# A graph layer in three blocks: message and node stages joined, and four operations moved

## Chip, cores and metric
The kernel runs on one core of a Trainium2 chip. The metric is the device time of one execution in microseconds, the median of several runs. Trainium2's engines work in parallel and meet at semaphores: PE (TensorE, matmuls and transposes), DVE (VectorE), ACT (ScalarE), POOL (GpSimd) and SP (SyncE, which here only starts DMAs). Each runs its own instructions strictly in the order written.

## What is computed
```python
h = maximum(layernorm(x), 0)                      # x: 50000 x 256
Q, K, V = h @ Wq, h @ Wk, h @ Wv                  # 8 heads of 32
scores = einsum('ehd,ehd->eh', Q[dst], K[src]) * SCALE    # 12500 edges, sorted by dst
w = exp(scores - max over the edges of a dst);  w = w / (sum over them + 1e-8)
out[dst] += V[src] * w
out = layernorm(h + out @ Wo_w + Wo_b, g1, b1)
ffn = gelu(out @ ffn_w1 + ffn_b1) @ ffn_w2 + ffn_b2       # 256 -> 512 -> 256
return x + layernorm(out + ffn, g2, b2)
```

## The kernel before
All numbers are float32. For accuracy a matmul of float32 data is done as three of fp32r data: each operand is split into a high part (a rounded copy, mostly made on ACT) and a low part (the difference, made on DVE), and hi*hi, hi*lo and lo*hi are summed in PSUM.

**Score stage** (`score_stage`). 25 groups of 512 edges. POOL gathers the rows of x for the dst side ("d") and src side ("s") by indirect DMA; DVE takes statistics (`statistics`, `inverse_root`), ACT normalises, PE transposes into the PSUM tile a_T, ACT and DVE split (`high_part`, `low_part`), PE forms Q, K and V. `products` and `head_sums` on DVE make the scores. V stays in SBUF as `vt`. a_T serves both sides in turn, so PE's transposes of side 1 wait for `low_part` of side 0. SP also fills agg_scratch in HBM with the bias of Wo.

**Softmax stage** (`softmax_stage`): scans over the sorted edges, untouched by the change.

**Message stage** (`message_stage`). 25 groups of 512 edges. SP loads alpha (the weights, 16 rows) and cont (does this edge continue its dst?); ACT casts alpha (L652); PE spreads it over the head dimensions into c_A (L587); DVE multiplies by vt (L632) and sums within a dst by a scan (L639); PE multiplies the totals by Wo (L599); ACT copies to c_rows (L657), four buffers; POOL scatters the rows to agg_scratch, four indirect DMAs a group (L682). The block ends when every scatter has landed.

**Node stage** (`node_stage`), a block of its own. First weights and vectors are loaded (L764 to L767), the weights are scaled and split on DVE (L845 to L852). Then 98 groups of 512 nodes; step s of the loop works on several groups at once:
- POOL adds agg_scratch to z of group s+3 by an accumulating DMA (L806), and b2 to x (L807); it makes u = zn*g1 + b1 + fb2 for group s+1 (L813, L815) and the reciprocal roots (L802, L828).
- ACT normalises z of group s+1 to zn (L943) and x of group s+4 with ReLU (L954); for group s it applies gelu in PSUM to the four chunks c of 128 hidden features (L963), makes act_hi (L968), seeds Y with u (L985); for group s+1 it makes zt_hi, the high part of the transposed zn, in two halves (L973).
- PE: for group s four chunks of six d_F matmuls (L1031), then the transposes of group s+1, half 0 (L1018), the d_Y matmuls of chunks 0 and 1 (L1042), the transposes of half 1, the d_Y matmuls of chunks 2 and 3. d_F has three banks, so chunk 3 takes the bank of chunk 0 and waits for act_lo 0; T is one bank, so half 1 waits for zt_lo 0.
- DVE: statistics (L887, L890), centring (L894) and output (L879) of group s-1; act_lo of group s (L857), zt_lo of group s+1 (L863); statistics of z for s+2 (L900, L909) and x for s+5 (L904, L913, L918).

The order of all of this is written out by hand in the loops over s.

Of the kernel before, what the change touches and what calls it, by code (L numbers as in the profile page):

```python
# [18 lines left out]
P = 128  # L19
# [70 lines left out]
def score_stage(nc, x, ends_cols, wq, wk, wv, wo_b, vt, score_dram, agg_dram):  # L90
    with ExitStack() as ctx:
# [56 lines left out]
        with nc.Block() as block:  # L148
# [38 lines left out]
            def _(dve):  # L187
# [68 lines left out]
                for s in range(FIRST, EG):  # L256
# [7 lines left out]
                    else:  # L264
                        statistics(s + 2)
                        products(s)
                        head_sums(s)
                        low_part(s + 1, 0)
# [251 lines left out]
def message_stage(nc, dst_cols, next_cols, wo, wo_b, vt, alpha_dram, cont_dram, agg_dram):  # L520
    with ExitStack() as ctx:
# [10 lines left out]
        w = sb("c_wo", [P, KD, D])  # L532
# [7 lines left out]
        msg = [sb(f"c_msg{r}", [P, KD, GR]) for r in range(2)]  # L540
        total = [sb(f"c_total{r}", [P, KD, GR]) for r in range(2)]
        rows = [sb(f"c_rows{r}", [P, GT, D]) for r in range(4)]
        A = [ctx.enter_context(nc.psum_tensor(f"c_A{r}", [P, KD, GR], f32)) for r in range(2)]
        Y = [ctx.enter_context(nc.psum_tensor(f"c_Y{r}", [P, GT, D], f32)) for r in range(2)]
# [7 lines left out]
        FIRST = -3  # L552
        with nc.Block() as block:
            @block.sync
            def _(sp):
                sp.dma_start(dst[:], dst_cols).then_inc(loaded, 16)
                sp.dma_start(nxt[:], next_cols).then_inc(loaded, 16)
                sp.dma_start(w[:], wo.rearrange("(k p) n -> p k n", p=P)).then_inc(loaded, 16)
# [11 lines left out]
                for c in range(FIRST, EG):  # L570
                    step(Step(c))

            @block.tensor
            def _(pe):
# [4 lines left out]
                def step(s):  # L579
# [9 lines left out]
                    if s.exists(EG):  # L589
# [7 lines left out]
                        for j in range(GT):  # L597
                            for k in range(KD):
                                ins = nc.tensor.matmul(Y[r][:, j, :], total[r][:, k, j * P:(j + 1) * P], w[:, k, :],  # L599
                                                       start=False, stop=(k == KD - 1), skip_group_check=True)  # L600
                        ins.then_inc(y_done, 1)
                for c in range(FIRST, EG):
                    step(Step(c))

            @block.vector
            def _(dve):

                dve.wait_ge(loaded, 64)
                nc.vector.tensor_tensor(same[:], dst[:], nxt[:], ALU.is_equal).then_inc(same_done, 1)
                dve.wait_ge(same_done, 1)  # L610
                nc.vector.scalar_tensor_tensor(row_of[:], same[:], float(SKIP), dst[:], ALU.mult, ALU.add)\
                    .then_inc(index_done, 1)
                dve.wait_ge(consts, 9)
                nc.vector.tensor_tensor(spread[:], spread_part[0][:], spread_part[1][:], ALU.add).then_inc(prep, 1)
                nc.vector.tensor_copy(ones[:], ones_raw[:]).then_inc(prep, 1)
                nc.vector.tensor_copy(bias_hi[:], bias_raw[:]).then_inc(prep, 1)
                dve.wait_ge(prep, 3)
                nc.vector.tensor_tensor(bias_raw[:], bias_raw[:], bias_hi[:].bitcast(f32), ALU.subtract).then_inc(prep, 1)
                nc.vector.tensor_scalar(bias_part[:], bias_hi[:].bitcast(f32), pick[:, 0:1], None, ALU.mult).then_inc(prep, 1)
                dve.wait_ge(prep, 5)  # L620
                nc.vector.scalar_tensor_tensor(bias[:], bias_raw[:], pick[:, 1:2], bias_part[:], ALU.mult, ALU.add)\
                    .then_inc(prep, 1)

                def step(s):
                    if s.exists(EG):
                        r = s.c % 2
                        dve.wait_ge(group_in[s.c % 4], s.use(4, 32))
                        if s.after(2):
                            dve.wait_ge(y_done, s.times(1, -1))
                        for c in range(KD):  # L630
# [10 lines left out]
                for c in range(0, EG):  # L641
                    step(Step(c))
# [466 lines left out]
```

## Time and profile before
| | us |
|---|---|
| median of 3 runs | 1828.78 (1828.08 to 1831.19) |
| the profiled execution | 1828.51 |
| its span, first to last instruction | 1826.8 |
| PE busy in it | 1650.9 (90%) |
| DVE | 1515.3 (83%) |
| POOL | 1295.5 (71%) |
| ACT | 1280.9 (70%) |

The score stage takes the first 310 us or so, the softmax until 362, the messages until 534, the nodes the rest. Busy shares are averages over these stages. Matmuls are pipelined and overlap in the records: PE counts as busy from one to the next if the gap is short, so the start-to-start spacing says more than the share.

### The profile page before, as it was taken

What the parts mean: (1) busy time and instruction counts of PE and PEld (TensorE: products, weight loads), DVE (VectorE), ACT (ScalarE), POOL (GpSimd) and SP (SyncE); (2) the same over time, 40 slices, a digit from 0 to 9 for tenths busy, and PEclk for the clock granted to TensorE, in tenths of its full rate; (3) what the DMA queues carried; (4) which work ended last, traced back from release to release, by engine and by line L of the source; (5) the groups of instructions that cost most, each with busy time, mean ns of one, the idle gap of its engine ahead of it and who ended that gap; (6) DMA issues with size and microseconds to landing.
All of it is one profiled execution on the core that took longest, in us unless ns stands there. A gap on an engine that the chain in (4) does not pass through costs nothing.

```text
span 1826.8 us, 31063 instructions
## 1 busy us (share of the span) xinstructions
PE 1650.9 (90%) x10411; PEld 1441.2 (79%) x10411; DVE 1515.3 (83%) x4604; ACT 1280.9 (70%) x2366; POOL 1295.5 (71%) x1313
## 2 busy tenths in 40 slices
PE   4899997299803999999999999999999999999997
PEld 4888887167702888888888888888888888888886
DVE  3888885677503899999999999999999999999986
ACT  3777775022203888888888888888888888888884
POOL 7777640057734777878878778778778778788783
PEclk8999999589955999999999999999999999999999
DMA  5899895034326677767777777777777677677761
GB/s 161 263 299 303 292 267 196 26 101 135 113 86 167 135 165 171 170 167 166 173 168 162 176 171 162 171 174 164 167 171 170 165 169 170 167 165 173 169 129 57
DMA packets 133619, 309.48 MB, mean 169 GB/s; under 512 B 14622, under 2 KB 69614, under 8 KB 133460
## 3 DMA queue, kind: packets, MB, share of 16 engines
q0 software_dynamic: 42624, 139.33, 37.8%
q1 hardware_dynamic: 90836, 168.17, 27.6%
q8 instruction: 83, 1.36, 0.3%
q14 instruction: 76, 0.62, 0.1%
HBM read 140.66 MB, written 118.20 MB: 142 GB/s over the span
## 4 chain that ended last, share of the span: by engine, by line
PE 67%; DMA 1%; DVE 1%; POOL 1%; ACT 0%; SPq 0%; issue 0%; DVEq 0%; POOLq 0%; ACTq 0%
PE d_F L1031 31%; PE d_Y L1042 31%; PE d_T L1018 6%; DMA d_fb_row<-in_fb 1%; PE d_Y L1008 0%; DMA d_z<-agg_scratch 0%; ACT d_zn L943 0%; PE d_F L1001 0%; SPq L767 0%; POOL d_zx_rstd L828 0%; POOL d_u L815 0%; POOL d_u L813 0%; ACT d_z L954 0%; DVE d_y_stats L887 0%; DVE d_zx_stats L900 0%
## 5 line engine op out<-in xcount | busy, mean ns | idle before, releaser
L1042 PE MATMUL d_Y<-d_w_hi,d_act_hi 128*128 128x256 f32 x1568 | 458.1, 292 | 0.0
L1042 PE MATMUL d_Y<-d_w_lo,d_act_hi 128*128 128x256 f32 x1568 | 441.5, 282 | 0.0
L1042 PE MATMUL d_Y<-d_w_hi,d_act_lo 128*128 128x256 f32 x1568 | 441.1, 281 | 0.0
L943 ACT ACTIVATE d_zn<-d_z,d_zx_nmr,d_zx_rstd 128x256 f32<-128x256 f32 x392 | 224.2, 596 | 151.1 <-POOL d_zx_nmr L831 151.1
L1031 PE MATMUL d_F<-d_zt_hi,d_w_hi 128*128 128x512 f32 x784 | 321.1, 410 | 2.0 <-DVE d_zt_lo L863 1.4
L1031 PE MATMUL d_F<-d_zt_hi,d_w_lo 128*128 128x512 f32 x784 | 310.1, 396 | 0.0
L1031 PE MATMUL d_F<-d_zt_lo,d_w_hi 128*128 128x512 f32 x784 | 310.0, 395 | 0.0
L963 ACT ACTIVATE d_F<-d_F,d_fb_col 128x512 f32<-128x512 f32 x392 | 259.5, 662 | 59.2 <-PE d_F L1031 59.0
L813 POOL TENSOR_TENSOR d_u<-d_zn,d_g_row 128x1024 f32<-128x1024 f32 x98 | 293.8, 2998 | 6.0 <-ACT d_zn L943 6.0
L1042 PEld LDWEIGHTS d_Y<-d_w_hi,d_act_lo 128*128 128x128 f32 x1568 | 296.0, 189 | 0.0
L1042 PEld LDWEIGHTS d_Y<-d_w_hi,d_act_hi 128*128 128x128 f32 x1568 | 295.7, 189 | 0.0
L1042 PEld LDWEIGHTS d_Y<-d_w_lo,d_act_hi 128*128 128x128 f32 x1568 | 295.6, 188 | 0.0
L857 DVE TENSOR_TENSOR d_act_lo<-d_F,d_act_hi 128x512 fp32r<-128x512 f32 x392 | 265.7, 678 | 11.9 <-ACT d_act_hi L968 11.9
L954 ACT ACTIVATE d_z<-d_x,d_zx_nmr,d_zx_rstd 128x256 f32<-128x256 f32 x392 | 213.8, 608 | 63.4 <-PE d_Y L1008 61.1
L815 POOL TENSOR_TENSOR d_u<-d_u,d_res_row 128x1024 f32<-128x1024 f32 x98 | 235.0, 2397 | 7.7
L968 ACT ACTIVATE d_act_hi<-d_F 128x512 fp32r<-128x512 f32 x392 | 234.7, 599 | 3.2
L887 DVE BATCH_NORM_STATS2 d_y_stats<-d_Y 128x6 f32<-128x256 f32 x392 | 139.7, 419 | 74.3 <-PE d_Y L1042 74.3
L1031 PEld LDWEIGHTS d_F<-d_zt_hi,d_w_hi 128*128 128x128 f32 x784 | 147.9, 189 | 61.4 <-DVE d_act_lo L857 34.2
L1031 PEld LDWEIGHTS d_F<-d_zt_hi,d_w_lo 128*128 128x128 f32 x784 | 148.2, 189 | 34.8
L799 POOL TENSOR_SCALAR d_y_veps<-d_y_mv 128x4 f32<-128x4 f32 x98 | 19.5, 199 | 217.6 <-DVE d_y_mv L890 217.6
L828 POOL TENSOR_TENSOR d_zx_rstd<-d_zx_veps,d_mhalf 128x8 f32<-128x8 f32 (+1 forms) x101 | 164.3, 1627 | 8.4
L879 DVE SCALAR_TENSOR_TENSOR d_o<-d_Y,d_y_rstd,d_x 128x256 f32<-128x256 f32 x392 | 169.7, 475 | 0.0
(163 smaller groups left out, 3728.2 us busy)
## 6 DMA issues: line engine op xcount, KB each, us to landing
agg_scratch<-a_bias_row SPq DMA_DIRECT2D x50, 1024.0 KB
d_x<-in_x SPq DMA_DIRECT2D x98, 512.0 KB, 4.2
d_z<-agg_scratch POOLq DMA_DIRECT2D x98, 512.0 KB, 5.6
d_x<-d_b_wide POOLq DMA_DIRECT2D x98, 512.0 KB, 7.5
out<-d_o SPq DMA_DIRECT2D x98, 512.0 KB, 2.9
c_cont<-cont_scratch SPq DMA_DIRECT2D x25, 256.0 KB, 3.4
a_xd<-in_x,a_idx POOLq DMA_INDIRECT x100
a_xs<-in_x,a_idx POOLq DMA_INDIRECT x100
```

Source lines behind the costliest of these rows:

```text
L813: nc.gpsimd.tensor_tensor(u[g % 2][:], zn[g % 2][:], wide(g1_row), ALU.mult).then_inc(scaled, 1)
L815: nc.gpsimd.tensor_tensor(u[g % 2][:], u[g % 2][:], wide(res_row), ALU.add).then_inc(u_done, 1)
L828: nc.gpsimd.tensor_tensor(zx_rstd[:, r, part], zx_veps[:, r, part], mhalf[:, part], ALU.pow)\
L857: nc.vector.tensor_tensor(act_lo[:, c, :], FF[:, (KF * s + c) % FB, :], act_hi[:, c, :].bitcast(f32), ALU.subtract).then_inc(glo_done, 1)
L879: ins = nc.vector.scalar_tensor_tensor(o[yr][:, j, :], Y[yr][:, j, :], y_rstd[:, yr, j:j + 1], xt[y % XR][:, j, :], ALU.mult, ALU.add)
L887: nc.vector.bn_stats(y_stats[:, yr, j, :], Y[yr][:, j, :]).then_inc(ystats_done, 1)
L943: ins = nc.scalar.activation(zn[gz % 2][:, j, :], z[gz % ZR][:, j, :], ACT.Identity, bias=zx_nmr[:, at % NR, 0, j:j + 1], scale=zx_rstd[:, ...
L954: ins = nc.scalar.activation(z[gx % ZR][:, j, :], xt[gx % XR][:, j, :], ACT.Relu, bias=zx_nmr[:, at % NR, 1, j:j + 1], scale=zx_rstd[:, at ...
L963: nc.scalar.activation(bank, bank, ACT.Gelu, bias=fb1_col[:, c:c + 1]).then_inc(gelu_done, 1)
L968: nc.scalar.activation(act_hi[:, c, :], FF[:, (KF * s + c) % FB, :], ACT.Identity).then_inc(ghi_done, 1)
L1031: ins = nc.tensor.matmul(FF[:, turn % FB, :], w[:, k, c * P:(c + 1) * P], a[:, k, :], start=(k == 0 and p == 0), stop=(k == KD - 1 and p = ...
L1042: ins = nc.tensor.matmul(Y[s % 2][:, j, :], a[:, c, j * P:(j + 1) * P], w[:, c, :], start=False, stop=(c == KF - 1 and w is w2_lo), skip_g ...
```

## The change
The message and node stages become one block, `message_node_stage`. Their instructions on each engine follow one another with no block end between. Node tiles (x, z, zn, u, o, b2, raw weights) lie in places of `vt` whose messages are done; d_T and d_F are the four banks low_banks that c_A uses before. While messages run, SP loads the vectors (ahead of group 0's alpha), the weights after group 4, six x tiles and b2; DVE splits the weights behind groups 6 to 11, takes statistics of the first XE = 4 x tiles behind groups 13 to 16 and their inverse roots after; ACT makes their ReLU tiles behind groups 19 to 22. The node loop starts at s = -3 instead of -6. The two waits for opening Y and the matmuls L1008 go; PE runs HEAT = 48 matmuls after the weights; ACT runs one gelu beforehand. The b2 add is issued for group s+2, not s+3. In the score stage `head_sums` goes behind `low_part(s + 1, 0)`. In the node step: half of the centring goes behind act_lo 0, act_hi 0 ahead of a norm, zt_hi 0 ahead of gelu 3, zt_lo 0 ahead of act_lo 2, one x statistic of the second pair ahead of zt_lo 0 and the other behind act_lo 2.

```diff
@@ score_stage, DVE
                         products(s)
+                        low_part(s + 1, 0)
                         head_sums(s)
-                        low_part(s + 1, 0)
@@ message_node_stage
+        XE = 4
+        X_FREE = (5, 6, 7, 9, 11, 13)
+        flat = vt[:].rearrange("p k e -> p (k e)")
...
-        FIRST, LAST = -6, NG + 1
+        FIRST, LAST = -3, NG + 1
+        HEAT = 48
@@ SP
                 for to, of in vectors:
                     sp.dma_start(to[:], of).then_inc(w_in, 16)
+                for c in range(-3, EG):
+                    step(Step(c))
+                    if c == 4:
+                        sp.wait_ge(msg_done, KD * 4)
+                        sp.dma_start(w1_raw, ...)
+                        sp.dma_start(w2_raw, ...)
+                    if c in X_FREE:
+                        g = X_FREE.index(c)
+                        sp.wait_ge(msg_done, KD * c)
+                        sp.dma_start(xt[g], rows_of(x, g)).then_inc(x_in[g], 16)
+                    if c == 16:
+                        sp.wait_ge(msg_done, KD * 16)
+                        sp.dma_start(b2_wide, b2_of).then_inc(b2_row_in, 16)
@@ PE, behind the messages
+                for n in range(HEAT):
+                    nc.tensor.matmul(FF[:, 2, :], w1_hi[:, 0, 0:P], w1_hi[:, n % KD, :], start=True, stop=True)
@@ DVE
+                for c in range(0, EG):
+                    step(Step(c))
+                    if 6 <= c < 12:
+                        weights(c - 6)
+                    if 13 <= c < 13 + XE:
+                        early_statistics(c - 13)
+                    if c == 13 + XE:
+                        dve.wait_ge(emv_done, XE * GT)
+                        nc.vector.tensor_scalar(e_veps[:], e_mv[:, :, :, 1], LN_EPS, None, ALU.add).then_inc(e_veps_done, 1)
+                    if c == 13 + XE + 1:
+                        early_root()
...
+                    centre((0, 1))
                     low_part(s, 0)
+                    centre((2, 3))
...
+                    if late(gx):
+                        nc.vector.bn_stats(zx_stats[:, r, 1, 2, :], xt[gx % XR][:, 2, :]).then_inc(xstats_done, 1)
+                    z_low_part(s + 1, 0)
                     low_part(s, 2)
...
-                    z_low_part(s + 1, 0)
                     low_part(s, 3)
@@ ACT
                     gelu(0)
-                    norm_z((2,))
                     high_part(0)
+                    norm_z((2,))
...
                     high_part(2)
-                    gelu(3)
                     z_high_part(0)
+                    gelu(3)
                     high_part(3)
@@ POOL
                         pool.dma_start(z[g % ZR], rows_of(agg_dram, g), accum_op=ALU.add).then_inc(agg_in[g % ZR], 16)
+                    g = s + 2
+                    if there(g):
+                        pool.dma_start(xt[g % XR], b2_wide, accum_op=ALU.add).then_inc(b2_in[g % XR], 16)
```

On DVE, one node step before, from the centring of the output to zt_lo 0 (the fourth act_lo follows):
```order
L894 SCALAR_TENSOR_TENSOR d_Y1<-d_Y1,d_y_mv,d_g2_row 128x256 x4
L857 TENSOR_TENSOR d_act_lo<-d_F,d_act_hi 128x512
L900 BN_STATS d_zx_stats<-d_z2 128x6 x4
L904 BN_STATS d_zx_stats<-d_x5 128x6 x2
L857 TENSOR_TENSOR d_act_lo<-d_F,d_act_hi 128x512
L909 BN_AGGR d_zx_mv<-d_zx_stats 128x2 x4
L913 BN_STATS d_zx_stats<-d_x5 128x6 x2
L857 TENSOR_TENSOR d_act_lo<-d_F,d_act_hi 128x512
L918 BN_AGGR d_zx_mv<-d_zx_stats 128x2 x4
L863 TENSOR_TENSOR d_zt_lo<-d_T,d_zt_hi 128x512
```

The same stretch of DVE now, up to the fourth act_lo (low_banks stands for d_F and d_T, vt for z and x; act_lo is L866, zt_lo is L872):
```order
L883 SCALAR_TENSOR_TENSOR Y1<-Y1,d_y_mv,d_g2_row 128x256 x2
L866 TENSOR_TENSOR d_act_lo<-low_banks,d_act_hi 128x512
L883 SCALAR_TENSOR_TENSOR Y1<-Y1,d_y_mv,d_g2_row 128x256 x2
L914 BN_STATS d_zx_stats<-vt 128x6 x4
L918 BN_STATS d_zx_stats<-vt 128x6 x2
L866 TENSOR_TENSOR d_act_lo<-low_banks,d_act_hi 128x512
L923 BN_AGGR d_zx_mv<-d_zx_stats 128x2 x4
L926 BN_STATS d_zx_stats<-vt 128x6
L872 TENSOR_TENSOR d_zt_lo<-low_banks,d_zt_hi 128x512
L866 TENSOR_TENSOR d_act_lo<-low_banks,d_act_hi 128x512
L930 BN_STATS d_zx_stats<-vt 128x6
L933 BN_AGGR d_zx_mv<-d_zx_stats 128x2 x4
```

The centring is in two halves around the first d_act_lo, and d_zt_lo has passed the third d_act_lo and the aggregate of x; one x statistic now stands on either side of the two.

On ACT, in the same step before, from the first gelu (L963) to the last d_act_hi (L968):
```order
L963 ACTIVATE d_F<-d_F,d_fb1_col 128x512
L943 ACTIVATE d_zn1<-d_z1,d_zx_nmr,d_zx_rstd 128x256
L968 ACTIVATE d_act_hi<-d_F 128x512
L963 ACTIVATE d_F<-d_F,d_fb1_col 128x512
L943 ACTIVATE d_zn1<-d_z1,d_zx_nmr,d_zx_rstd 128x256
L985 ACTIVATE d_Y0<-d_u0 128x1024
L968 ACTIVATE d_act_hi<-d_F 128x512
L963 ACTIVATE d_F<-d_F,d_fb1_col 128x512
L968 ACTIVATE d_act_hi<-d_F 128x512
L963 ACTIVATE d_F<-d_F,d_fb1_col 128x512
L973 ACTIVATE d_zt_hi<-d_T 128x512
L968 ACTIVATE d_act_hi<-d_F 128x512
```

The same stretch of ACT now (gelu is L999, act_hi L1004, zt_hi L1009, the norm of z L979, the seed of Y L1021):
```order
L999 ACTIVATE low_banks<-low_banks,d_fb1_col 128x512
L1004 ACTIVATE d_act_hi<-low_banks 128x512
L979 ACTIVATE vt<-vt,d_zx_nmr,d_zx_rstd 128x256
L999 ACTIVATE low_banks<-low_banks,d_fb1_col 128x512
L979 ACTIVATE vt<-vt,d_zx_nmr,d_zx_rstd 128x256
L1021 ACTIVATE Y0<-vt 128x1024
L1004 ACTIVATE d_act_hi<-low_banks 128x512
L999 ACTIVATE low_banks<-low_banks,d_fb1_col 128x512
L1004 ACTIVATE d_act_hi<-low_banks 128x512
L1009 ACTIVATE d_zt_hi<-low_banks 128x512
L999 ACTIVATE low_banks<-low_banks,d_fb1_col 128x512
L1004 ACTIVATE d_act_hi<-low_banks 128x512
```

The first act_hi has passed the third norm of z, and zt_hi has passed the last gelu.

On SP, at the start of the message stage, as it is now, from the last of its own constants to the loads of group 0:
```order
L643 DMA c_bias_raw<-in_wo_b 2x256
L655 DMA d_g1_col<-in_g1_col 128x2
L655 DMA d_b1_col<-in_b1_col 128x2
L655 DMA d_fb1_col<-in_fb1_col 128x4
L655 DMA d_g2_row<-in_g2 128x256
L655 DMA d_g1_row<-in_g1 128x256
L655 DMA d_res_row<-in_b1 128x256
L655 DMA d_fb2_row<-in_fb2 128x256
L651 DMA c_alpha_in0<-alpha_scratch 16x512
L652 DMA c_cont0<-cont_scratch 128x512
```

Before, c_alpha_in0 and c_cont0 followed c_bias_raw directly; the seven d_ rows are the vectors of the node stage.

## Rows read from the trace of the kernel before

**Rows 1.** Stretch, length, busy: PE, weight loads, DVE, ACT, POOL; granted clock; DMA share; GB/s.
```profile
1000.00:1500.00 500.00, 500.00 (x3194) 438.70 (x3193) 468.88 (x1519) 416.35 (x760) 401.38 (x400) 1.00 0.72 169
505.00:510.00 5.00, 0.00 (x0) 0.00 (x0) 0.00 (x0) 1.01 (x1) 3.88 (x4) 0.50 0.27 98
```

**Rows 2.** Chain that ended last: start us, us, what; node stage.
```profile
603.93 5.74 PE d_F L1031 x24
...
1793.13 5.75 PE d_F L1031 x24
1805.45 5.76 PE d_F L1031 x24
```

**Rows 3.** PE in order of time, one middle step: start us, us, instruction.
```profile
1095.90 0.39 PE L1031 MATMUL d_F<-d_zt_lo,d_w_hi 128*128 128x512 f32 x1
1096.14 0.40 PE L1031 MATMUL d_F<-d_zt_hi,d_w_lo 128*128 128x512 f32 x1
1096.45 0.50 PE L1031 MATMUL d_F<-d_zt_hi,d_w_hi 128*128 128x512 f32 x1
1096.79 0.39 PE L1031 MATMUL d_F<-d_zt_lo,d_w_hi 128*128 128x512 f32 x1
...
1101.10 0.28 PE L1042 MATMUL d_Y<-d_w_lo,d_act_hi 128*128 128x256 f32 x1
1101.38 0.66 PE L1018 MATMUL d_T<-d_ident,d_zn 128*128 128x128 f32 x4
```

**Rows 4.** PE in a late step, at the transposes of half 1.
```profile
1789.57 0.28 PE L1042 MATMUL d_Y<-d_w_lo,d_act_hi 128*128 128x256 f32 x1
1789.69 0.60 PE L1018 MATMUL d_T<-d_ident,d_zn 128*128 128x128 f32 x4
```

**Rows 5.** ACT and DVE in the middle step of rows 3.
```profile
1094.85 0.59 ACT L968 ACTIVATE d_act_hi<-d_F 128x512 fp32r<-128x512 f32 x1
1095.71 0.68 DVE L857 TENSOR_TENSOR d_act_lo<-d_F,d_act_hi 128x512 fp32r<-128x512 f32 x1
1099.59 0.60 ACT L973 ACTIVATE d_zt_hi<-d_T 128x512 fp32r<-128x512 f32 x1
1100.67 0.66 DVE L863 TENSOR_TENSOR d_zt_lo<-d_T,d_zt_hi 128x512 fp32r<-128x512 f32 x1
```

**Rows 6.** PE in order of time, one score step.
```profile
267.31 0.40 PE L356 MATMUL a_K<-a_hts_hi,a_wv_lo 128*128 128x512 f32 x1
...
268.02 0.41 PE L368 MATMUL a_T<-a_ident,a_hs 128*128 128x128 f32 x2 [0.31 <-DVE a_htd_lo L253]
```

**Rows 7.** Last scatter, landing of the scatters, the path to the first d_F.
```profile
523.28 0.99 POOL L682 DMA_INDIRECT agg_scratch<-c_rows,c_row_of  x1 [0.30 <-issue]
DMA to landing us min/median/max: 2.1/2.8/4.3
569.65 1.03 POOL L806 DMA_DIRECT2D d_z<-agg_scratch  x1 [2.82 <-ACT d_z L954]
576.69 0.65 DVE d_zx_stats L904 x2
588.42 0.79 PE L1031 MATMUL d_F<-d_zt_hi,d_w_hi 128*128 128x512 f32 x1 [1.41 <-DVE d_zt_lo L863]
```

**Rows 8.** Start of the message stage, and the slowest vector load of the node block.
```profile
364.11 0.32 SPq L567 DMA_DIRECT2D c_alpha_in<-alpha_scratch  x1
368.42 0.62 ACT L652 CAST c_alpha<-c_alpha_in 16x512 fp32r<-16x512 f32 x1 [31.34 <-DMA c_cont<-cont_scratch]
...
538.63 13.26 DMA d_fb_row<-in_fb
```

**Rows 9.** A scan and a scatter in order of time; all scatters by line.
```profile
486.43 1.27 DVE L639 TENSOR_TENSOR_SCAN c_total<-c_cont,c_total,c_msg 128x512 f32<-128x512 f32 x1
486.60 1.91 POOL L682 DMA_INDIRECT agg_scratch<-c_rows,c_row_of  x1 [0.30 <-issue]
...
L682 POOL DMA_INDIRECT agg_scratch<-c_rows,c_row_of x100 | 112.3, 1123 | 46.9 <-issue 29.2 <-ACT c_rows L657 17.1 <-DMA agg_scratch<-c_rows,c_row_of 0.6
```

## What I predict, before any run of the changed kernel

> **What bounds the kernel now.** I read first where each engine is busy over time, then the chain of work that ended last, then single steps in order of time. In the middle of the node stage (the last 1200 us) PE is busy without a gap, 500.00 of 500 us, at the full granted clock; DVE has 468.88, ACT 416.35, POOL 401.38 [rows 1]. The chain says the same: the run of 24 d_F matmuls that opens a node step starts at 603.93 in the second step and at 1805.45 in the last, 96 steps of (1805.45-603.93)/96 = 12.52 us. Yet the last step but one takes only 1805.45-1793.13 = 12.32 [rows 2]. So a "full" PE still holds about 0.2 us that is not work: a busy share cannot show this, start-to-start spacing can.
>
> In one middle step d_F matmuls follow each other every 0.24 us (1095.90 to 1096.14), but the first of the fourth hidden chunk comes after 0.31 and the one behind it after 0.34 [rows 3]. This chunk reuses the PSUM bank of chunk 0, so it waits for act_lo 0. That subtraction starts on DVE at 1095.71, lasts 0.68, and ends at 1096.39, while act_hi 0 started on ACT at 1094.85 and took 0.59 [rows 5]: DVE was still centring the four row tiles of the output before. The second stall is at the transposes of half 1: last d_Y matmul 1101.10, transposes 1101.38, 0.28 later [rows 3]; near the end of the program the same pair is 0.12 apart [rows 4]. They share the one bank T with half 0 and wait for zt_lo 0, which runs 1100.67 to 1101.33 and needs zt_hi 0 of 1099.59 [rows 5].
>
> Three other places: (1) in the score stage the transposes of the source side start at 268.02 though the last matmul before them started at 267.31, with a wait of 0.31 for a_htd_lo, which on DVE stands behind the reduction of the products [rows 6]. (2) The last scatter is issued at 523.28 and mostly lands 2.8 us after issue, but the first read-and-add of agg_scratch is issued at 569.65 and the first d_F starts at 588.42 [rows 7]; between lie the end of one block, the loads of the next, the weight split and the first four norms. (3) The message stage is paced by POOL: 100 scatters at 0.99 + 0.30 us and a surplus (112.3 us instead of 99) [rows 7, 9].
>
> **The change, part by part.** The profiled execution took 1828.51 us for a span of 1826.8; the median of the runs is 1828.78, so I work from 1828.5.
>
> Score stage. Low part 0 goes ahead of the reduction. The transposes could follow the matmul of 267.31 at its 0.24 spacing, at 267.55 instead of 268.02: 0.47 us per step [rows 6], for the 23 steps that use the new order and have a next group: 10.8 us. The reduction is then late by two subtractions, but its reader, the transpose of the sums, stands behind eight transposes. Bounds 0 and 10.8, the first if the gathers or ACT pace the stage; I take -10.8.
>
> Start of the message stage. SP now issues seven vector loads ahead of the first alpha and cont. Before, alpha 0 was issued at 364.11 and ACT began on it at 368.42 [rows 8]. Nothing hides this: POOL's scatters begin later by the same amount, and POOL sets the pace. The issues alone, each like the 0.4 us between neighbouring ones, cost about 3; the same vectors in the old node block landed up to 13.26 us after issue [rows 8]. I take +5, nearer the low end since there the FFN weights and the wide b2 were queued among them; ends 3 and 13.
>
> Middle of the message stage. DVE gets the weight split (groups 6 to 11) and statistics of four x tiles (13 to 16), ACT the early ReLUs, SP eight large loads. DVE and ACT run ahead of POOL by up to four groups, so their own time is covered; once this cover is gone each microsecond counts in full. What is not covered is what DVE does to POOL's descriptors: a scan on DVE starts at 486.43, and the scatter issued at 486.60 takes 1.91 instead of 0.99 us [rows 9]. Six weight pieces could each do this once more: 6 x 0.92 = 5.5. They could as well move POOL out of step with the scans and save from the 112.3 - 99 = 13 us of surplus. I take +3; ends -13 and +5.5. The Trainium skill, "SBUF — State Buffer", section "SBUF: two separate sides", says that VectorE and GpSimd share a port pair held for a whole instruction by an operation in a two-port mode or with two SBUF inputs, and that descriptors of GpSimd's DMAs cannot be written meanwhile. The scan has two SBUF inputs, and its row agrees. By this rule the copies and differences of the weights speak against the change, and the sum would take the +5.5 end, 2.5 us more than mine.
>
> From the last scatter to the first d_F. Weights, constants, x tiles and four ReLU tiles are ready by then, so POOL may issue the read of agg_scratch as soon as its scatters have landed: 523.28 + 2.8 to 4.3 is 526.1 to 527.6 [rows 7]; I take 526.5. No block ends here any more. The path from that issue to d_F was 588.42-569.65 = 18.8 us; two pairs of x statistics of 0.65 leave it for group 0 [rows 7], 17.5 remain. d_F would start at 544.0 instead of 588.42: -44.4. If the landing were as slow as the slowest one shown, 13.26 [rows 8], it would be -34; the smaller POOL work of the first groups and the ACT table load moved ahead may add -2. I count -1 of that.
> The 48 HEAT matmuls run while the scatters drain and cost nothing, but bring nothing either: with PE idle in 505 to 510 the granted clock is 0.50 (the 1.2 GHz level) [rows 1]. After the HEAT matmuls PE waits for the landing, the statistics and the norm, over 10 us, so I expect the first d_F at the low level as before. The Trainium skill, "TensorE: Matmul & The Clock Gate", section "What's actually happening", has the clock fall back after an idle stretch, and the row agrees; were the clock kept up, the first 12 matmuls would take 0.24 us each and not twice that, 2.9 us less.
>
> Node step. act_lo 0 goes behind two of the four centrings and act_hi 0 ahead of one norm. It then starts some 0.7 us earlier, and PE wants it only at 1096.38: the fourth chunk loses 0.31+0.34-2x0.24 = 0.17 us of delay [rows 3], rounded to 0.18 with the spacing before. zt_hi 0 moves ahead of gelu 3 (about 0.5 us earlier), zt_lo 0 ahead of act_lo 2 (about 0.9 earlier): the transposes no longer wait, which is the 0.20 between 12.52 and the 12.32 of a late step [rows 2, 4]. Sum 0.38 a step, 12.14 left; 96 x 0.38 = 36.5 us.
> What is late next? act_lo 2 now stands behind zt_lo 0 (0.67) and one x tile less (0.35), with DVE's new waits about 0.6 us later than today, which is about when the transposes of half 1 start; PE wants it 0.35 us later: met, narrowly. act_lo 3, zt_lo 1 and the seed of Y have at least as much. ACT pays about 0.1 us twice, since an act_hi right behind its own gelu must wait for that to finish; DVE then waits about 0.2 us for act_hi 0 and 0.1 for zt_hi 0. DVE's work is 468.88/500 x 12.52 = 11.74 a step, so 0.4 us of slack holds these 0.3 barely. POOL and ACT are a loop (norm, u, reciprocal root, norm), and POOL's 401.38/500 x 12.52 = 10.05 leaves it 2 us. Postponing the b2 add by one group keeps the same number of transfers per step; the result needs it two steps later.
>
> Sum: 1828.5 - 10.8 + 5 + 3 - 44.4 - 1 - 36.5 = 1743.8, **1744 us**.
>
> **Rivals.**
> A. Another loop takes over in the node step. DVE needs 11.74 plus new waits; with 0.3 of waits and some jitter the period could stop at 12.33, as in late steps. For it: DVE is at 94% [rows 1]. Against: a DVE that is late finds its waits on ACT already over. Half of the 36.5 goes: 1762. If nothing at all is gained, 1780.
> B. The scatters are stretched by the weight pieces, or the group-0 loads arrive at the 13 us end, or the scatters land late: each about +8 to 10, time 1753. For it: rows 8 and 9. Against: only six groups of 25 are touched.
> C. Slower than before. The new order on DVE makes act_lo 2 and 3 wait for zt_hi 0, hence for PE's transposes of half 0, hence for the fourth d_F chunk; if that closes into a loop, every step pays. The rest of the change wins 44.4+1+10.8-8 = 48.2 us, so it decides only from 48.2/96 = 0.5 us a step over today's 12.52, a step of 13.02 or more; at 13.2 the time is 1828.5-48.2+96x0.68 = 1846. Against: zt_hi 0 starts at 1099.59 today [rows 5] and moves half a microsecond up, so DVE reaches zt_lo 0 at most 0.1 us too early, and ACT, with 416.35/500 x 12.52 = 10.4 us of work a step [rows 1], catches up.
> D. The change does less than it says: no cover for the loads in the message stage, so that half of the 44.4 comes back: 1766. Against: POOL's rows are four groups deep.
>
> **How the numbers follow.** Forecast 0.62, A 0.18 (0.04 of it without any gain in the node step), B 0.13, C 0.03, D 0.04. The forecast's own cases reach from 1730 (both message costs absent) to 1752. To take in B and the middle of A the range is 1729 to 1768. A measurement of this kernel can tell about 0.2%, 3.7 us, from no change: faster 0.96, same 0.01, slower 0.03.
>
> **What would show it.** Node step: d_F runs every 12.1 to 12.2 us, no 0.31 and 0.34 spacing at the fourth chunk, transposes of half 1 0.12 behind the last d_Y. End of the message stage: first d_z read about 3 us behind the last scatter, first d_F 17 to 18 us later, at half clock. Start: the first c_alpha cast about 5 us later against the start of its stage. Score stage: 10.4 instead of 10.9 us per group. The forecast is wrong if d_F steps stay above 12.3, if the stretch between first and last scatter grows by over 6 us, or if the gap from last scatter to first d_F exceeds 28 us.

## The result, and the profile after

The changed kernel takes 1735.51 us (1734.87 to 1736.3, 4 runs) where the kernel before takes 1828.48: a ratio of 0.9489, with an interval of 0.9472 to 0.9505. I had said 1744, with a range of 1729 to 1768. The profiled execution took 1736.3 us for a span of 1734.6. All traces used below are of fast executions but that of e4_old_score_order, a slow one (1890.23 us, the other four of that kernel 1861.22 to 1867.34), from which only the length of a node step is taken.

The middle of the node stage, in the same columns as [rows 1]:

```profile
1000.00:1500.00 500.00, 500.00 (x3302) 452.68 (x3302) 490.44 (x1573) 438.30 (x786) 415.39 (x416) 1.00 0.74 175
505.00:510.00 5.00, 5.00 (x24) 4.14 (x23) 0.00 (x0) 0.00 (x0) 3.78 (x5) 1.00 0.23 92
```

PE is "full" as before, but with 3302 matmuls in place of 3194 in the same 500 us. DVE has risen from 94% to 98%. The second row lies within the HEAT matmuls.

The chain that ended last, from the last scatter to the second node step, and the last full step (start us, us, what), answers to [rows 2, 7]:

```profile
519.89 2.10 DMA agg_scratch<-c_rows,c_row_of
...
522.29 5.57 DMA vt<-agg_scratch
...
528.30 1.40 DVE d_zx_stats L914 x4
...
534.18 1.13 PE low_banks L737 x4
...
539.24 7.52 PE low_banks L750 x24
...
553.25 5.60 PE low_banks L750 x24
558.85 0.44 PE low_banks L737 x4
559.28 2.81 PE Y L761 x24
562.09 0.44 PE low_banks L737 x4
562.53 2.81 PE Y L761 x24
...
1713.57 5.60 PE low_banks L750 x24
```

The steps are (1713.57-553.25)/96 = 12.087 us apart instead of 12.516. The pieces of one step add up to it: 5.60+0.44+2.81+0.44+2.81 = 12.10. No wait is left in PE's chain.

PE at the transposes of half 1 of a middle step, to be held against [rows 3, 4]:

```profile
1009.02 0.28 PE L761 MATMUL Y<-d_w_lo,d_act_hi 128*128 128x256 f32 x1
1009.14 0.60 PE L737 MATMUL low_banks<-d_ident,vt 128*128 128x128 f32 x4
```

The transposes start 0.12 us behind the start of the last matmul of Y; before it was 0.28.

DVE in the same step:

```profile
1002.23 0.89 DVE L883 SCALAR_TENSOR_TENSOR Y<-Y,d_y_mv,d_g_row 128x256 f32<-128x256 f32 x2
1003.22 0.69 DVE L866 TENSOR_TENSOR d_act_lo<-low_banks,d_act_hi 128x512 fp32r<-128x512 f32 x1
...
1007.88 0.69 DVE L872 TENSOR_TENSOR d_zt_lo<-low_banks,d_zt_hi 128x512 fp32r<-128x512 f32 x1
```

Where the 92.2 us of span went, by stretches of the two traces:

| stretch | before | after | difference | I had said |
|---|---|---|---|---|
| start to the first load of the message stage | 362.4 | 349.5 | -12.9 | -10.8 |
| that load to the first scatter | 19.5 | 25.8 | +6.3 | +5 |
| first to last scatter | 141.4 | 144.6 | +3.2 | +3 |
| last scatter to first d_F | 65.1 | 19.35 | -45.8 | -44.4, -1 with the next row |
| first to second d_F | 15.5 | 14.0 | -1.5 | |
| 96 node steps | 12.516 each | 12.087 each | -41.2 | -36.5 |
| end | | | -0.3 | 0 |

### The profile page after: what moved, and what is told of

The parts are those of the page before. It is cut to its first block, busy times and chain, and to the rows that moved or that the text cites. A ratio compares the mean times of both kernels' runs of the same rounds, so it can differ in the third digit from the quotient of the medians.

```text
span 1734.6 us, 31133 instructions
## 1 busy us (share of the span) xinstructions
PE 1614.0 (93%) x10451; PEld 1448.6 (84%) x10451; DVE 1526.0 (88%) x4610; ACT 1299.2 (75%) x2369; POOL 1293.8 (75%) x1301
## 4 chain that ended last, share of the span: by engine, by line
PE 68%; POOL 1%; DMA 0%; DVE 0%; issue 0%; ACT 0%; DVEq 0%; POOLq 0%; ACTq 0%
PE low_banks L750 32%; PE Y L761 32%; PE low_banks L737 5%; POOL agg_scratch L1060 1%; DMA vt<-agg_scratch 0%; DMA agg_scratch<-c_rows,c_row_of 0%; ACT vt L979 0%; DVE d_y_stats L903 0%; DVE d_zt_lo L872 0%; DVE d_zx_stats L914 0%; ACT d_zt_hi L1009 0%; DVE vt L895 0%; DVE Y L883 0%; POOL d_zx_rstd L1105 0%; DVEq L637 0%
## 5 line engine op out<-in xcount | busy, mean ns | idle before, releaser
L761 PE MATMUL Y<-d_w_hi,d_act_hi 128*128 128x256 f32 x1568 | 455.2, 290 | 0.0
L761 PE MATMUL Y<-d_w_hi,d_act_lo 128*128 128x256 f32 x1568 | 437.8, 279 | 0.0
L761 PE MATMUL Y<-d_w_lo,d_act_hi 128*128 128x256 f32 x1568 | 437.2, 279 | 0.0
L979 ACT ACTIVATE vt<-vt,d_zx_nmr,d_zx_rstd 128x256 f32<-128x256 f32 x392 | 224.2, 596 | 154.0 <-POOL d_zx_nmr L1108 154.0
L750 PE MATMUL low_banks<-d_zt_hi,d_w_hi 128*128 128x512 f32 x784 | 310.7, 396 | 1.4 <-DVE d_zt_lo L872 1.4
L750 PE MATMUL low_banks<-d_zt_lo,d_w_hi 128*128 128x512 f32 x784 | 310.9, 397 | 0.0
L750 PE MATMUL low_banks<-d_zt_hi,d_w_lo 128*128 128x512 f32 x784 | 310.6, 396 | 0.0
L761 PEld LDWEIGHTS Y<-d_w_hi,d_act_lo 128*128 128x128 f32 x1568 | 295.3, 188 | 0.0
L761 PEld LDWEIGHTS Y<-d_w_hi,d_act_hi 128*128 128x128 f32 x1568 | 295.2, 188 | 0.0
L761 PEld LDWEIGHTS Y<-d_w_lo,d_act_hi 128*128 128x128 f32 x1568 | 294.8, 188 | 0.0
L866 DVE TENSOR_TENSOR d_act_lo<-low_banks,d_act_hi 128x512 fp32r<-128x512 f32 x392 | 265.6, 678 | 19.0 <-ACT d_act_hi L1004 9.5
L999 ACT ACTIVATE low_banks<-low_banks,d_fb_col 128x512 f32<-128x512 f32 x392 | 259.2, 661 | 16.3 <-PE low_banks L750 7.0
L1004 ACT ACTIVATE d_act_hi<-low_banks 128x512 fp32r<-128x512 f32 x392 | 234.4, 598 | 9.3
L990 ACT ACTIVATE vt<-vt,d_zx_nmr,d_zx_rstd 128x256 f32<-128x256 f32 x376 | 204.9, 595 | 0.0
```

Of the source, the lines that this page charges most:

```text
L750: ins = nc.tensor.matmul(FF[:, turn % FB, :], w[:, k, c * P:(c + 1) * P], a[:, k, :], start=(k == 0 and p == 0), stop=(k == KD - 1 and p = ...
L761: ins = nc.tensor.matmul(Y[s % 2][:, j, :], a[:, c, j * P:(j + 1) * P], w[:, c, :], start=False, stop=(c == KF - 1 and w is w2_lo), skip_g ...
L866: nc.vector.tensor_tensor(act_lo[:, c, :], FF[:, (KF * s + c) % FB, :], act_hi[:, c, :].bitcast(f32), ALU.subtract).then_inc(glo_done, 1)
L979: ins = nc.scalar.activation(zn[gz % 2][:, j, :], z[gz % ZR][:, j, :], ACT.Identity, bias=zx_nmr[:, at % NR, 0, j:j + 1], scale=zx_rstd[:, ...
L990: ins = nc.scalar.activation(z[gx % ZR][:, j, :], xt[gx % XR][:, j, :], ACT.Relu, bias=zx_nmr[:, at % NR, 1, j:j + 1], scale=zx_rstd[:, at ...
L999: nc.scalar.activation(bank, bank, ACT.Gelu, bias=fb1_col[:, c:c + 1]).then_inc(gelu_done, 1)
```

## The experiments

Four of them (e1 to e4) ran on a chip on which the kernel before takes 1946.79 us: in e1 a group of the score stage takes (414.6-69.5)/24 = 14.4 us, against 10.5 in the changed kernel above, and the scatters take 150.4 us from first to last against 144.6. So I compare the lengths of their node steps and the time from the first d_F to the end, not their times. The other eight ran where the kernel before takes 1829.1 to 1829.2, and are compared in full.

### The node orders, undone one by one

**e1_old_node_order**: everything of the change stays, but DVE and ACT do the node step in the old order.

```diff
                     centre((0, 1))
+                    centre((2, 3))
                     low_part(s, 0)
-                    centre((2, 3))
...
-                        nc.vector.bn_stats(zx_stats[:, r, 1, 2, :], xt[gx % XR][:, 2, :]).then_inc(xstats_done, 1)
-                    z_low_part(s + 1, 0)
+                        for j in range(2, GT):
+                            nc.vector.bn_stats(zx_stats[:, r, 1, j, :], xt[gx % XR][:, j, :]).then_inc(xstats_done, 1)
                     low_part(s, 2)
                     if late(gx):
-                        nc.vector.bn_stats(zx_stats[:, r, 1, 3, :], xt[gx % XR][:, 3, :]).then_inc(xstats_done, 1)
...
+                    z_low_part(s + 1, 0)
                     low_part(s, 3)
...
+                    norm_z((2,))
                     high_part(0)
-                    norm_z((2,))
...
+                    gelu(3)
                     z_high_part(0)
-                    gelu(3)
```

> The changed kernel (1735.5 us) with the node step of DVE and ACT in the order of before; all else as changed. My theory: the two stalls of PE (fourth d_F chunk, transposes of half 1) are what the orders removed, so d_F runs come every 12.52 us again instead of 12.09, 96 x 0.43 = 41 us more: 1776 to 1778. Rival (part of the 0.43 comes from the joined block itself, its tiles in vt or its banks): the step is 12.2 to 12.4, 1745 to 1765.

Measured: ratio 0.9758 (0.9742 to 0.9774), 1899.16 us there; step 12.48 us. From the first d_F to the end of the span 1893.3-660.2 = 1233.1 us; the changed kernel has 1734.6-539.24 = 1195.4. The orders are worth 37.7 us in the joined kernel. I had expected 41 us and a step of 12.52: 0.04 us a step does not come back with the old orders.

**e2_old_act_order**: only the first two of these pieces, act_lo 0 and act_hi 0, as before; zt_hi 0 and zt_lo 0 stay early.

> Only act_lo 0 goes behind all four centrings again, and act_hi 0 behind the third norm; zt_hi 0 and zt_lo 0 stay ahead. My theory: the two stalls are independent, this brings back the one at the fourth d_F chunk, 0.18 us a step, 97 steps: 18 us more, 1753. Rival 1 (DVE has no slack, so the step length is set by its sum and the place of act_lo 0 does not matter): 1736. Rival 2 (either stall alone sets the step): 1770 or more.

Measured: ratio 0.9645 (0.9626 to 0.9664); step (1859.29-683.93)/96 = 12.24 us, d_F x24 5.75 in place of 5.60. First d_F to end: 1880.4-670.0 = 1210.4, or 15.0 more than the changed kernel. Given the early zt_lo 0, the place of act_lo 0 is worth 0.15 a step, close to what the spacing at the fourth chunk had said (0.17, [rows 3]).

**e3_old_zt_order**: only the last two, zt_hi 0 and zt_lo 0, as before, and with zt_lo 0 the x statistic that had moved behind it; act_lo 0 stays mid-centring.

> Only zt_hi 0 goes behind gelu 3 and zt_lo 0 behind act_lo 2 again; act_lo 0 stays in the middle of the centring. My theory: the stall at the transposes of half 1 comes back, 0.22 us a step: 21 us more, 1757. Rival (the earlier act_lo 0 moves everything on DVE enough that zt_lo 0 is in time anyway): 1736 to 1740.

Measured: ratio 0.9867 (0.985 to 0.9883); step 12.69 us, first d_F to end 1921.8-670.5 = 1251.3. This is worse than both orders undone. I had expected 0.22 us a step over the changed kernel, 21 us in all; it is 0.60, and 55.9 us to the end, and against e1 the step is 0.21 longer. The chain of one step (start us, us, what) shows why:

```profile
1012.03 2.81 PE Y L761 x24
1014.84 1.41 PE low_banks L750 x6
...
1016.27 0.67 ACT low_banks L999
...
1016.97 0.61 ACT d_act_hi L1004
...
1017.60 0.69 DVE d_act_lo L866
1018.29 0.79 DVE Y L883 x2
1019.08 1.30 DVE d_zx_stats L914 x4
...
1023.14 0.22 DVE d_zx_mv L932 x3
1023.36 0.66 DVE d_zt_lo L872
...
1024.06 0.66 PE low_banks L737 x4
```

This is one loop: the last half of Y, the first chunk of d_F, gelu 0 and act_hi 0 on ACT, DVE's work from act_lo 0 to zt_lo 0 back to back, the transposes, Y again. A second way leads from Y straight to DVE: statistics from 1014.88, and two centrings of 0.395 us from 1016.61 that end at 1017.40. It is the shorter by 0.20 us, since act_lo 0 starts only at 1017.60. With zt_lo 0 behind act_lo 2 DVE has no slack behind act_lo 0, so these 0.20 us of waiting for act_hi 0 count in full.

**e11_act_hi_alone** tests that reading: e3 with act_lo 0 back behind all four centrings, so that DVE no longer waits for act_hi 0. ACT's order stays as in e3.

> The changed kernel with the old place of act_lo 0 (behind all four centrings) and of zt_hi 0 and zt_lo 0; only act_hi 0 stays ahead of the third normalisation. With act_lo 0 mid-centring as well the step was 12.69 us, with nothing moved 12.48. Theory: what made the step longer is VectorE's wait for act_hi 0 in the middle of the centrings (0.12 us), in a loop in which VectorE has no slack between the last matmul of Y and zt_lo 0. Behind four centrings act_hi 0 is long there: step 12.48 to 12.50 us. Rival: it is ScalarE's order (the third normalisation behind act_hi 0) that makes the loop longer: step 12.65 us or more.

Measured: 1774.0 us (1772.91 to 1774.46), ratio 0.9695 (0.968 to 0.971). Its step, on DVE:

```profile
1015.72 1.42 DVE L903 BATCH_NORM_STATS2 d_y_stats<-Y 128x6 f32<-128x256 f32 x4 [0.61 <-PE Y L761]
...
1017.45 1.67 DVE L883 SCALAR_TENSOR_TENSOR Y<-Y,d_y_mv,d_g_row 128x256 f32<-128x256 f32 x4
1019.03 0.68 DVE L866 TENSOR_TENSOR d_act_lo<-low_banks,d_act_hi 128x512 fp32r<-128x512 f32 x1
...
1023.99 0.65 DVE L872 TENSOR_TENSOR d_zt_lo<-low_banks,d_zt_hi 128x512 fp32r<-128x512 f32 x1
```

No wait stands ahead of act_lo 0, and the next d_y_stats begins at 1028.19: a step of 12.47, as with everything old (1772.7-539.6 = 1233.1 to the end, exactly e1's). The loop here is the second way of e3. So act_hi 0 ahead of a norm does nothing by itself, and act_lo 0 mid-centring costs 0.21 a step where the zt order is old, which is the wait of 0.20. Where zt_lo 0 is early it gains 0.15.

### The score order

**e4_old_score_order** and, on the other chip, **e9_old_score_again** are one kernel: head_sums(s) ahead of low_part(s + 1, 0), as before.

```diff
-                        low_part(s + 1, 0)
                         head_sums(s)
+                        low_part(s + 1, 0)
```

> Only head_sums goes ahead of low_part(s + 1, 0) in the score stage again. My theory: 0.5 us for each of 23 groups comes back, 12 us: 1747.5, with 10.9 instead of 10.35 us per group. Rival (the gathers have sped up for another reason, e.g. the state of the memory): 1736, 10.35 us per group.

Measured: 1866.2 us, ratio 0.9583 (0.9567 to 0.9599). No run of the changed kernel stood beside it on that chip, whose score groups are longer anyway, so this told nothing of the order. Its node step, (1867.50-707.17)/96 = 12.087 us, is that of the changed kernel, so node steps do not differ between the two chips.

> The changed kernel with one edit undone: in the score stage the low half of the next group's first tile stands behind the head sums again, as before. Theory: the score group goes back from 10.34 to 10.84 us, so the message stage's first load is issued at about 362 us in place of 349.5 and the time is 1735.5 + 12.5 = 1748 us (1746 to 1750). Rival: the 12.9 us came from something else in the joined block (an earlier load, a shorter tail of the softmax); then the groups stay at 10.34 and the time at 1735 to 1737.

Measured: 1748.33 us (1747.41 to 1749.15), 12.8 more than the changed kernel; the first load of the message stage goes from 349.5 back to 361.9. The rows of the score group's one matmul for the sums (duration ns min/median/max, first and last start), e9 and then the changed kernel:

```profile
L400 PE MATMUL a_S<-a_ident,a_cols x25: 272/273/284, 46.1 to 310.1; 128*32 128x128 f32 x25
```

```profile
L400 PE MATMUL a_S<-a_ident,a_cols x25: 272/273/421, 46.4 to 297.8; 128*32 128x128 f32 x25
```

264.0/24 = 11.00 us a group against 251.4/24 = 10.48. PE in one score step of the changed kernel, to be held against [rows 6]:

```profile
257.00 0.40 PE L356 MATMUL a_K<-a_hts_hi,a_wv_lo 128*128 128x512 f32 x1
257.23 1.04 PE L368 MATMUL a_T<-a_ident,a_hs 128*128 128x128 f32 x8
```

The transposes follow after 0.23 us; before it was 0.71, with a wait for a_htd_lo.

### The joined block

**e10_orders_only**: the kernel before with all the orders of the change, and two blocks.

> The kernel before, with only the orders changed (score order, act_lo 0 mid-centring, act_hi 0 ahead of the third normalisation, zt_hi 0 ahead of gelu 3, zt_lo 0 ahead of act_lo 2); the two blocks stay apart. Theory that the parts add up: 1828.5 - 12.9 for the score order - 41.2 for 96 node steps = 1774.5 us, so the joined block is worth 39 us by itself (1771 to 1778). Rival: the orders need the joined block's other layout and gain less in the old one: 1785 or more.

Measured: 1780.09 us (1779.03 to 1781.35), ratio 0.9731 (0.9717 to 0.9744). So the orders give 49.0 us and the joined block 44.6 more. This is above the 1771 to 1778 that I had expected and below the 1785 of the rival: the node step is longer than the changed kernel's. Its pieces:

```profile
1004.15 5.58 PE d_F L1036 x24
...
1010.16 2.85 PE d_Y L1047 x24
...
1013.44 2.85 PE d_Y L1047 x24
1016.29 5.58 PE d_F L1036 x24
```

1016.29-1004.15 = 12.14 us here, (1757.24-591.16)/96 = 12.147 over all steps. Two runs of 24 Y matmuls take 2.85 in place of 2.81, d_F 5.58 in place of 5.60, and there is no wait in any. The orders give 12.516-12.147 = 0.37 a step; 0.06 a step, nearly 6 us in all, comes only with the joined block. All twelve traces with the joined block have runs of Y of 2.81 (a few of 2.83 or 2.84), both traces without it have 2.85. The last 48 Y matmuls of the program, here and in the changed kernel:

```profile
1762.82 5.77 PE d_Y L1047 x48
```

```profile
1719.17 5.61 PE Y L761 x48
```

POOL is idle in these stretches, the DMA share is 0.16 and 0.14, and the difference is still there. So it does not come from POOL's work or from heavy transfers beside the matmuls. Its cause is open.

By the stretches of the table, e10 against the changed kernel, the joined block costs 6.0 us at the start of the message stage and 1.8 between the scatters, and gives 44.2 between the last scatter and the first d_F, 1.1 in the first step and 5.8 in the other 96.

**e5_late_vectors**: the loads of the vectors on SP behind the alpha and cont loads of groups 0 to 3, not ahead of alpha 0.

```diff
-                for to, of in vectors:
-                    sp.dma_start(to[:], of).then_inc(w_in, 16)
                 for c in range(-3, EG):
                     step(Step(c))
+                    if c == 0:
+                        for to, of in vectors:
+                            sp.dma_start(to[:], of).then_inc(w_in, 16)
```

> SP issues the seven vector loads of the node part behind the alpha and cont loads of groups 0 to 3 instead of ahead of them. My theory: the message stage then starts as before, first scatter 19.4 instead of 25.8 us behind the first load of the stage, and since POOL paces the stage all of it comes back: 1729.5, 6 us less. Rival (the 6 us come from the cold clock of PE and from elsewhere): within 1 us of 1735.5.

Measured: 1731.31 us (1729.01 to 1732.0), ratio 0.9459 (0.9446 to 0.9472). ACT's first cast of alpha in the changed kernel, and then here:

```profile
360.63 0.62 ACT L948 CAST c_alpha<-c_alpha_in 16x512 fp32r<-16x512 f32 x1 [36.43 <-DMA c_cont<-cont_scratch]
```

```profile
355.27 0.62 ACT L949 CAST c_alpha<-c_alpha_in 16x512 fp32r<-16x512 f32 x1 [31.67 <-DMA c_cont<-cont_scratch]
```

It starts 5.4 us earlier, as does, within 0.1, the first scatter (369.95 against 375.26). 0.6 of this is a message stage that begins earlier in this run (first load at 348.9, not 349.5), so from first load to first scatter the loads cost 4.7: 21.0 us are left of 25.8, and 4.2 reach the end. I had expected 19.4, as in the kernel before, and 6 us. Most of what stays is on PE behind the first alpha. The 16 matmuls by Wo of the first group, before and in the changed kernel:

```profile
374.50 5.39 PE L599 MATMUL c_Y<-c_wo,c_total 128*128 128x256 f32 x16
```

```profile
367.00 6.30 PE L713 MATMUL Y<-c_wo,c_total 128*128 128x256 f32 x16
```

Between the two levels of 0.50 and 1.00 the granted clock is 0.68 in the mean over the first of these stretches and 0.58 over the second; in e5 the same 16 take 6.64 us at 0.55.

**e8_late_weights**: the six weight pieces of DVE behind the last group instead of behind groups 6 to 11.

> The six pieces of the weight split run on DVE behind group 24 instead of behind groups 6 to 11. My theory (a scatter's descriptors wait for DVE instructions with two SBUF inputs or a fast copy): the lengthened scatters among groups 4 to 9 go back to the pattern of before, and the pieces, 5 us of DVE in a row while the last scatters are issued, lengthen 3 to 5 of those instead. First to last scatter 141 to 146 us instead of 144.6, time 1732 to 1736. Rival (the 3.2 us that this stretch grew come from the x loads or the early statistics): no piece lengthens a scatter, first to last 144 to 145.

Measured: 1734.96 us (1734.16 to 1735.48), ratio 0.9483 (0.947 to 0.9496): no difference. In the changed kernel single pieces do lengthen scatters. A difference of the weights on DVE, and the scatters around it:

```profile
406.15 1.20 DVE L820 TENSOR_TENSOR d_w_lo<-vt,d_w_hi 128x1024 fp32r<-128x1024 f32 x1
```

```profile
404.55 1.30 POOL L1060 DMA_INDIRECT agg_scratch<-c_rows,c_row_of  x1 [0.30 <-issue]
406.16 2.05 POOL L1060 DMA_INDIRECT agg_scratch<-c_rows,c_row_of  x1 [0.30 <-issue]
```

Yet with the pieces gone from there, scans fall on scatters instead. I take the scatters above 1.05 us, sum what each takes over 0.985, and see from the rows of DVE what ran beside it for over 0.1 us:

| | scatters above 1.05 | over 0.985, us | of it beside scans | beside weight pieces | first to last scatter |
|---|---|---|---|---|---|
| before | 15 | 13.5 | 13.5 | | 141.4 |
| e10 | 21 | 15.1 | 15.1 | | 142.8 |
| changed kernel | 22 | 16.8 | 13.5 | 3.2 | 144.6 |
| e8 | 20 | 17.5 | 16.2 | 1.3 | 145.2 |

The last column grows by about what the sum does.

### The HEAT matmuls

**e6_no_heat** (HEAT = 0) and **e7_long_heat** (HEAT = 134, which reaches to the first transposes).

> The 48 HEAT matmuls are left out; they write only to a bank that is overwritten. My theory: they end some 20 us before the first transpose, whose clock is 0.50 anyway, so the time stays 1735.5 within 0.5. Rival (they keep part of the warmth): about 3 us more.

> HEAT = 134 instead of 48, so that PE works until just before the first transposes. My theory: the clock is then 1.00 at the first transposes and d_F matmuls; these gain 1 + 2 us (4.1 instead of 6.0 us for the first 18 d_F), but the fourth chunk then waits for act_lo 0, which hangs on POOL's norm of group 1 and not on PE, so only 0.7 to 1.5 us stay: 1734 to 1735. Rival (PE alone sets the start): 3 us less, 1732.5. Should the heating overrun, 0 to 2 us more.

Measured: 1735.05 us (1733.9 to 1735.89) and 1733.71 (1733.59 to 1736.35). The stretch of the first d_F (columns as in rows 1), changed kernel, then long HEAT:

```profile
535.00:540.00 5.00, 2.17 (x8) 1.38 (x7) 2.00 (x7) 1.20 (x2) 4.77 (x5) 0.50 0.88 172
```

```profile
535.00:540.00 5.00, 3.69 (x16) 3.02 (x17) 0.69 (x1) 1.25 (x3) 4.75 (x7) 1.00 0.44 87
```

In the changed kernel the clock is 0.50 in every stretch from 520 to 540. 134 matmuls keep the clock at 1.00 (2.4 GHz) through the first d_F, and the time does not change beyond its spread, because PE then stands still for act_lo 0:

```profile
540.38 0.40 PE L750 MATMUL low_banks<-d_zt_hi,d_w_lo 128*128 128x512 f32 x1
542.32 0.50 PE L750 MATMUL low_banks<-d_zt_hi,d_w_hi 128*128 128x512 f32 x1 [1.55 <-DVE d_act_lo L866]
```

From the first d_F to the first Y matmul it takes 544.18-536.31 = 7.9 us here and 546.95-539.24 = 7.7 in the changed kernel at the low level. Only the way from the last scatter to the first d_F is shorter, 18.7 us against 19.35, through faster transposes. The chain that leads to act_lo 0 in e7 comes from POOL:

```profile
537.29 1.68 POOL d_zx_rstd L1105
...
539.28 1.09 ACT vt L979 x2
...
541.57 0.70 DVE d_act_lo L866
```

This is the reciprocal root of group 1, its norm, and gelu 0 and act_hi 0 behind them on ACT.

**e12_late_vectors_long_heat**: e5 and e7 together.

> Both helpful edits at once: the vectors' loads behind group 0, and 134 in place of 48 matmuls that keep TensorE busy until the first transposes. Theory: the vectors' loads gave 4 us (the message stage starts earlier) and the long run of matmuls 1 to 2 (the first step's 24 matmuls at full clock), and they are in different places, so they add up: 1729.5 us (1728 to 1731). Rival: the first step waits for act_lo and not for TensorE, so the clock gives nothing and the time is 1731 to 1732.

Measured: 1730.62 us (1728.24 to 1733.56), ratio 0.946 (0.9447 to 0.9474). The spreads of e5 and e12 overlap; the two statements were too close to be told apart by the time. The trace shows that this was no full test: the message stage started earlier while the drain stayed as long, the 134 matmuls had ended at 527.9, and in 530 to 535 the granted clock was 0.60. The late vectors are what gains; e5 and e12 beat the changed kernel by 4 to 5 us.

## Why the prediction was right

The mechanism was the one forecast, at every stretch of the table; none of the rivals came about. The sum was 7.5 us short on a span difference of 92.2.

One bound was added up wrongly: without the two costs of the message stage the sum gives 1743.8-8 = 1735.8, not the 1730 that I named.

**Score stage**, -10.8 said, -12.9 measured; e9 gives back 12.4 at the first load and 12.8 in the time. The transposes start at the spacing of the matmuls ahead of them, as said. I multiplied 0.47 by 23 steps; it is 0.52 between groups, over 24 intervals, so 10.8 was no bound.

**Start of the message stage**, +5 said, +6.3 measured. e5 shows that the vectors' loads make up 4.7 of it where the stage starts and 4.2 at the end. Most of the rest is the first group's matmuls at a lower granted clock (0.9 us in the 16 by Wo), which I had at nothing.

**Middle of the message stage**, +3 said, +3.2 measured. The size was right, and the reason only in part. The trace of the changed kernel has it as I weighed it: five pieces lengthen scatters by 3.2 us, and scans take 13.5 as before. A difference of the weights lengthens the scatter of 406.16 to 2.05 us. The Trainium skill ("SBUF — State Buffer", section "SBUF: two separate sides"), which I cited, limits the case of two SBUF inputs to a GpSimd instruction that reads SBUF, and names descriptors only for the two-port modes; I had left out both. The scatter reads its row numbers from SBUF, and its rows, 1.91 us beside a scan and 2.05 beside a difference, show the case of two SBUF inputs here. But I priced the pieces as an addition, and e8 shows that they are none: with them behind the last group the scans take 16.2. Extra length appears wherever scans and scatters fall on each other, and any change of DVE's timing moves that. Why they fall on each other more often in e8 and e10 than before is open.

**Last scatter to first d_F**, -44.4 said, -45.8 measured. The read of agg_scratch is issued 2.40 us behind the last scatter, d_F 16.95 behind that; I had said 3.2 and 17.5. The first step is 1.5 shorter, mainly since it no longer has ACT's table load in it (1.28 us at 591.76, in the chain of the kernel before); e10, which keeps the load, has 15.09 where the kernel before has 15.51 and the changed one 14.01. I had counted 1.

**HEAT**: nothing said, nothing measured, by e6. My reason for the loss of the clock was right: 0.50 in 520 to 540. That is what the clock gate's rule in the Trainium skill ("TensorE: Matmul & The Clock Gate", section "What's actually happening") says, and the rows agree. But I had put 2.9 us on a clock that is kept. e7 shows 1.7 on the first 18 d_F matmuls (4.07 us from the first start to the last, against 5.73), and that act_lo 0 takes it back, 1.55 us at one matmul: the first step is bound by the way through POOL, ACT and DVE.

**Node step**, 0.38 said, 0.43 measured, and the largest part of the miss: 41.2 instead of 36.5 us. e10 has the orders without the joined block and gives 0.37, a step of 12.147 us. The other 0.06 comes with the joined block and sits in the spacing of the Y matmuls (24 in 2.81 against 2.85). I did not foresee it and no run names its cause; e1 against the kernel before (12.48 against 12.52) has the same sign.

**What was wrong inside that step** though its sum held: I took 0.18 for act_lo 0 and 0.20 for zt_lo 0 as two stalls that can be taken away one by one. With the four combinations side by side they are not:

| step, us | zt_lo 0 behind act_lo 2 | zt_lo 0 ahead of act_lo 2 |
|---|---|---|
| act_lo 0 behind four centrings | 12.48 (e1, e11) | 12.24 (e2) |
| act_lo 0 mid-centring | 12.69 (e3) | 12.087 |

The kernel before was held by a loop through DVE, the second way of e3; its trace says so in rows which I had not read, the waits of DVE in 1000 to 1500, and one of them in the step of [rows 3]:

```profile
DVE d_y_stats L887 <- PE d_Y L1042: 29.7, 40, 0.7
```

```profile
1092.39 1.43 DVE L887 BATCH_NORM_STATS2 d_y_stats<-d_Y 128x6 f32<-128x256 f32 x4 [0.74 <-PE d_Y L1042]
```

40 times in 500 us, once in every step, DVE had run out of work and stood 0.7 us for Y, while PE stood for zt_lo 0. That is the sign of a loop between two engines, though neither is idle much. It closes: DVE works from 1092.39 to the end of zt_lo 0 at 1101.33, the transposes follow from 1101.38 and take 0.66, the last half of Y takes 2.85, and the next d_y_stats starts at 1104.92, 12.53 us after the first. Moving zt_lo 0 up takes work out of the loop; only then does act_lo 0 decide anything. In the changed kernel DVE waits for Y twice in the 1150 us from 550 to 1700. Rival A, another loop that takes over, had its loop in the kernel before, not after, though not because DVE was full: DVE was idle 0.78 us a step there. The room that I allowed DVE ("holds these 0.3 barely") was right: its idle time is (500-490.44)/500 x 12.087 = 0.23 us a step, which is about the 0.20 wait ahead of act_lo 0 (two centrings from 1002.23 would end at 1003.02; it starts at 1003.22).

## What to carry to other kernels

A stall on a full engine is found by start-to-start spacing, but what it is worth depends on the loop it lies in: before adding up stalls, look for an engine that waits once per step for the engine that waits for it, and follow that loop. Reorderings on one engine are to be tried together as well as one by one, since one that loses alone (0.21 us a step here) can gain beside another (0.15). Joining two stages pays what lies between them (44.2 us here), but loads hoisted to its front go behind the ones that the first stage waits for.

## What the runs showed of the hardware that I had not expected

The same 24 Y matmuls without any wait take 2.85 us in one program and 2.81 in another (e10 and the changed kernel), which with d_F makes 0.06 us a step, 0.5% of it, and nearly 6 us in all. The clock was granted at 1.00 in both, and with POOL idle 48 of them still took 5.77 and 5.61.

A scatter of 0.99 us takes up to 2.05 when an instruction of DVE with two SBUF inputs runs beside it; taking the six weight pieces away from there (e8) did not shorten the sum (17.5 us, not 16.8), for more scans came to lie beside scatters.

One chip takes 1946.79 us for a program that takes 1829.1 on another, and node steps agree: 12.087 us for one kernel on both (e4 and e9). What differs is the score stage with its gathers, 14.4 us a group against 10.5 and a first group that ends 23 us later (e1 and the changed kernel), and the message stage, 150.4 us against 144.6 from first to last scatter.
